# Flamingo layer with a mixture of experts: the up products of the routed experts take the rows' high and low parts in one product

## What is computed

```python
x = x + tanh(g_xattn) * cross_attention(layernorm(x), ctx, Wq, Wk, Wv)
h = layernorm(x)
top, ids = top_k(h @ router_w.T, 1)
xs = h * sigmoid(top)
for e in range(8):
    g, u = split(xs @ w_gate_up[e])
    routed = where(ids == e, (silu(g) * u) @ w_down[e], routed)
x = x + tanh(g_ffn) * (routed + shared_expert(h))
```

## Time and profile before

| | us |
|---|---|
| median of 3 runs | 973.37 (971.97 to 973.90) |
| profiled execution | 973.49 |
| its span in the profile | 971.3 |
| TensorE busy in the span | 944.4 |
| VectorE busy | 628.1 |
| ScalarE busy | 548.8 |
| first gate product of unit 0 starts at | 699.0 |

### The profile page before, as it was taken

One profiled execution on the slowest core, in us unless ns is written; L12 is line 12 of the kernel. 1 busy time (PEld: TensorE's weight loads), 2 busy tenths in 40 slices (PEclk: granted clock), 3 DMA queues, 4 the chain that ended last, 5 costly groups with the idle time before them and its releaser, 6 DMA issues. The chain is left out here.

```text
span 971.3 us, 24842 instructions
## 1 busy us (share of the span) xinstructions
PE 944.4 (97%) x10541; PEld 782.7 (81%) x10541; DVE 628.1 (65%) x1461; ACT 548.8 (57%) x839; POOL 171.6 (18%) x206
## 2 busy tenths in 40 slices
PE   5899999999999999999889999999999999999997
PEld 4677777777777777777777998999988888988886
DVE  6877755867558656676666444344577777777774
ACT  5477766777676777676732121221356666666653
POOL 1002121121112122112242300000111122112111
PEclk9999999999999999999999999999999999999999
DMA  8454544655435745354552310011386787677762
GB/s 314 109 104 99 92 101 93 134 104 97 98 94 132 158 80 116 79 107 127 113 141 94 91 34 32 22 44 57 123 258 214 235 242 233 211 232 243 229 202 64
DMA packets 175403, 129.98 MB, mean 134 GB/s; under 512 B 114610, under 2 KB 152498, under 8 KB 175288
## 3 DMA queue, kind: packets, MB, share of 16 engines
q1 hardware_dynamic: 165864, 108.60, 43.3%
q0 software_dynamic: 6544, 16.46, 5.5%
q10 hardware_dynamic: 2880, 3.29, 1.0%
HBM read 88.79 MB, written 13.56 MB: 105 GB/s over the span
## 5 line engine op out<-in xcount | busy, mean ns | idle before, releaser
L583 PE MATMUL bank<-arena_f32r 128*128 128x512 f32 (+1 forms) x1308 | 331.8, 403 | 12.4 <-DVE arena_f32r L946 12.0
L583 PEld LDWEIGHTS bank<-arena_f32r 128*128 128x128 f32 (+1 forms) x1308 | 231.9, 184 | 75.4 <-DVE arena_f32r L898 10.6
L777 ACT ACTIVATE probs<-score_banks 128x1600 f32<-128x1600 f32 x96 | 144.9, 1509 | 46.5 <-PE score_banks L602 45.9
L1689 ACT ACTIVATE hT_hi<-arena_f 128x224 fp32r<-128x224 f32 (+2 forms) x96 | 42.3, 441 | 116.9 <-DVE arena_f L1700 116.9
L1628 PE MATMUL bank<-xnT,arena_f32r 128*128 128x224 f32 (+1 forms) x720 | 102.5, 293 | 0.0
L1628 PEld LDWEIGHTS bank<-xnT,arena_f32r 128*128 128x128 f32 x720 | 97.0, 190 | 1.8 <-issue 0.7
L1700 DVE TENSOR_TENSOR arena_f<-bank,arena_f 128x224 f32<-128x224 f32 (+2 forms) x93 | 41.2, 443 | 65.8 <-PE bank L1628 65.1
L617 PEld LDWEIGHTS bank<-probs,values 128*17 128x17 f32 (+1 forms) x3072 | 63.4, 97 | 23.4 <-issue 21.5
L617 PE MATMUL bank<-probs,values 128*17 128x100 f32 (+1 forms) x3072 | 78.8, 250 | 0.8 <-ACT probs L777 0.8
L1054 POOL TENSOR_TENSOR heads_out<-heads_out,inv_sum 100x256 f32<-100x256 f32 x30 | 30.3, 1010 | 209.2 <-DVE inv_sum L1017 209.2
L1590 DVE TENSOR_TENSOR arena_f32r<-arena_f,arena_f32r 128x1024 fp32r<-128x1024 f32 x43 | 52.6, 1224 | 18.8 <-ACT arena_f32r L1583 18.8
(11 more groups left out here) (282 smaller groups left out, 1803.7 us busy)
## 6 DMA issues: line engine op xcount, KB each, us to landing
arena_f<-L_ffn_w_gate_up SPq DMA_DIRECT2D x48, 512.0 KB, 4.0
arena_f<-L_ffn_w_down SPq DMA_DIRECT2D x24, 512.0 KB, 4.0
arena_f<-ctx SPq DMA_DIRECT2D x15, 722.0 KB, 4.2
w_raw<-L_ffn_w_gate_up SPq DMA_DIRECT2D x16, 512.0 KB, 3.8
w_raw<-L_ffn_w_down SPq DMA_DIRECT2D x8, 512.0 KB, 5.0
x_all<-x SPq DMA_DIRECT2D x8, 400.0 KB
x_rows<-x_all SPq DMA_DIRECT2D x4, 800.0 KB
x_all<-x_rows POOLq DMA_DIRECT2D x4, 768.0 KB, 6.5
```

The lines of the kernel that those rows point to most:

```text
L583: product = PE.matmul(bank[0:rows, :], src[:, j, 0:rows], weight, start=(m == 0), stop=(m == 11))
L777: A.activation(k.probs[n % 2][:], k.score_banks[:, :, 0:GH * k.N].rearrange("p j (r n) -> p j r n", r=GH), ACT.Exp, scale=float(HD) ** -0. ...
L1689: A.activation(k.hT[it % 2][0][:, j, 0:width], k.hidden[j][:, 0:width], ACT.Copy).then_inc(r.h_high, 1)
```

## The change

The up product gets the form of the gate product: `pe_expert_gate` becomes `pe_expert_gate_up` and is called for both. For each of the two blocks in a unit there are now a copy by ScalarE of the bank's second half to the tile `up_first` (`act_copy_up`), and an addition by VectorE (`dve_sum_up`); the multiplication reads `up_first` and not the bank (`dve_mult_expert`), and waits for the addition. `up_first` is one tile for both blocks, so the copy of a block waits for the multiplication before it (`r.mult`). The order on VectorE changes: the sums of block 1 come before the low part of block 0, and the residual addition moves from the end of quarter 0 to the middle of quarter 1. The rest of the diff takes cases out of `pe_gate_up` that its remaining callers in the shared stage don't have.

```diff
-def pe_expert_gate(k, r, PE, w, n, j):
+def pe_expert_gate_up(k, r, PE, w, n, j, which):
     it, u, xs = r.it0 + n, r.u0 + n, k.xn_both[n // k.NQ % 2]
-    bank = k.bank[product_bank(r, it, j, 0)]
-    high, low = (t[:].rearrange("p (k f) -> p k f", k=k.KD)[:, :, P * j:P * j + P] for t in k.w_split[u % 3][0])
-    w.wait_ge(r.w_low, 3 * u + 1)
+    bank = k.bank[product_bank(r, it, j, which)]
+    high, low = (t[:].rearrange("p (k f) -> p k f", k=k.KD)[:, :, P * j:P * j + P] for t in k.w_split[u % 3][which])
+    w.wait_ge(r.w_low, 3 * u + which + 1)
     if n:
-        w.wait_ge(r.gate_summed, 2 * n + j - 1)
+        w.wait_ge((r.gate_summed, r.up_summed)[which], 2 * n + j - 1)
     else:
-        w.wait_ge(r.silu, 2 * it)
+        w.wait_ge((r.silu, r.mult)[which], 2 * it)
...
+def act_copy_up(k, r, A, w, n, j):
+    it = r.it0 + n
+    w.wait_ge(r.gu, 4 * it + 2 * j + 2)
+    w.wait_ge(r.mult, 2 * it + j)
+    A.activation(k.up_first[:, 0:SLOTS], k.bank[product_bank(r, it, j, 1)][:, SLOTS:2 * SLOTS],
+                 ACT.Copy).then_inc(r.up_copied, 1)
...
+def dve_sum_up(k, r, V, w, n, j):
+    up = k.up_first[:, 0:SLOTS]
+    w.wait_ge(r.up_copied, 2 * n + j + 1)
+    V.tensor_tensor(up, k.bank[product_bank(r, r.it0 + n, j, 1)][:, 0:SLOTS], up, ADD).then_inc(r.up_summed, 1)
+
+
+def dve_mult_expert(k, r, V, w, n, j):
+    h, it = k.hidden[j][:, 0:SLOTS], r.it0 + n
+    w.wait_ge(r.silu, 2 * it + j + 1)
+    w.wait_ge(r.up_summed, 2 * n + j + 1)
+    V.tensor_tensor(h, k.up_first[:, 0:SLOTS], h, MULT).then_inc(r.mult, 1)
...
         for j in range(KF):
-            pe_expert_gate(k, r, PE, w, n, j)
-            pe_gate_up(k, r, PE, w, r.it0 + n, r.u0 + n, j, 1, k.xnT[e % 2], SLOTS)
+            for which in range(2):
+                pe_expert_gate_up(k, r, PE, w, n, j, which)
...
         act_copy_gate(k, r, A, w, n, 0)
         if a is not None:
             act_part_high(k, r, A, w, a)
+        act_copy_up(k, r, A, w, n, 0)
         act_silu_expert(k, r, A, w, n, 0)
         act_copy_gate(k, r, A, w, n, 1)
         act_h_high(k, r, A, w, r.it0 + n, 0, SLOTS)
+        act_copy_up(k, r, A, w, n, 1)
         if b is not None:
             act_part_high(k, r, A, w, b)
         act_silu_expert(k, r, A, w, n, 1)
...
         dve_sum_gate(k, r, V, w, n, 0)
         if a is not None:
             dve_part_low(k, r, V, w, a)
-        dve_mult(k, r, V, w, r.it0 + n, 0, SLOTS)
+        dve_sum_up(k, r, V, w, n, 0)
+        dve_mult_expert(k, r, V, w, n, 0)
+        dve_sum_gate(k, r, V, w, n, 1)
+        dve_sum_up(k, r, V, w, n, 1)
         dve_h_low(k, r, V, w, r.it0 + n, 0, SLOTS)
-        dve_sum_gate(k, r, V, w, n, 1)
         if b is not None:
             dve_part_low(k, r, V, w, b)
-        dve_mult(k, r, V, w, r.it0 + n, 1, SLOTS)
+        dve_mult_expert(k, r, V, w, n, 1)
+        if e and q == 1:
+            dve_add_residual(k, r, V, w, e - 1)
         dve_h_low(k, r, V, w, r.it0 + n, 1, SLOTS)
         if n == 0 and r is k.first:
             dve_shared_add(k, V, w, 15, shared_points(16))
         if c is not None:
             dve_part_low(k, r, V, w, c)
-        if n and q == 0:
-            dve_add_residual(k, r, V, w, e - 1)
```

More of the change, by code:

```diff
@@ L348, in sweep_semaphores @@
     r.gate_copied, r.gate_summed = sem(f"{name}_gate_copied"), sem(f"{name}_gate_summed")
+    r.up_copied, r.up_summed = sem(f"{name}_up_copied"), sem(f"{name}_up_summed")
     r.ids_in = sem(f"{name}_ids_in")
@@ L1607, in pe_gate_up @@
     taken = (r.silu, r.mult)[which]
-    if it < min(r.it0, CT) and j == 0:
+    if it < CT and j == 0:
         weight = [t[:] for t in k.w_first[which]]
@@ L1612, in pe_gate_up @@
         w.wait_ge(r.w_low, 3 * u + which + 1)
-    if r.it0 and it == 0:
+    if it == 0:
         if j == 0:
@@ L1617, in pe_gate_up @@
             w.wait_ge(k.first_copied, which + 1)
-    elif r.it0 and it == 1:
+    elif it == 1:
         w.wait_ge(k.exped, 6 * k.B)
-    elif it <= r.it0:
-        if r.it0 and it == 2:
+    else:
+        if it == 2:
             w.wait_ge(k.finish_v, 4)
-        w.wait_ge(taken, 2 * it + (j if it < r.it0 else 0))
-    else:
-        w.wait_ge(taken, 2 * it + j - 1)
+        w.wait_ge(taken, 2 * it + j)
     for i in range(k.KD * share // shares, k.KD * (share + 1) // shares):
@@ L2205, in sweep_again @@
     k.G.dma_reset()
-    for s in [r.w_high, r.w_low, r.gu, r.gate_copied, r.gate_summed, r.silu, r.mult, r.h_high, r.h_low, r.routed_down, r.ids_in, r.xt_turned,
+    for s in [r.w_high, r.w_low, r.gu, r.gate_copied, r.gate_summed, r.up_copied, r.up_summed, r.silu, r.mult, r.h_high, r.h_low, r.routed_down, r.ids_in, r.xt_turned,
               r.xt_high, r.xt_low, r.y_added, *r.w_in, *r.rows_in, *r.residual_in, *r.y_out]:
```

## The result

The changed kernel takes 979.80 us (median of 5 runs, 978.95 to 982.51) against 973.07 before: a ratio of 1.0072, 95% interval 1.0061 to 1.0083, so 6.7 us slower. (The 973.07 is the median of five runs; the 973.37 of the first three is within 0.3 of it.) The forecast was 976.6, slower, with a range of 971.5 to 980.5. The direction and the cause hold; the loss is twice what the sum gave.

What follows compares the result with a forecast made beforehand. TensorE bounds at 32.72 us per four units; after the change VectorE and ScalarE at 33.05 against 32.08. Last part b 3.3 us later, less 0.16 for shorter products: 3.2 on the profiled 973.49, less 0.12: 976.6 us, range 971.5 to 980.5.

Steps and rivals of the forecast that it cites:

- 1.1 us of room in four units: Routed stage before the change: VectorE's own pace is 31.6 us for four units, against TensorE's 32.72.
- The product is 0.08 us shorter: TensorE's up product in the gate's form: each costs 0.08 us less, 64 of them 5.1 us.
- The formula for the products' spacing: N / 2.4 + 2.5 ns for a TensorE product of N columns; estimated saving 0.6 us in all; profile row preferred.
- The second copy of up: ScalarE's block 1 copy between VectorE's multiplication and part b: 0.25 us more a round, bounds 0.24 and 0.36.
- 0.41 us for the sum of block 0: VectorE's up sum ahead of the multiplication: 0.38 + 0.03 us more a unit, bounds 0.30 and 0.46.
- The tail: After unit 31's last up product: the hidden values' low part is done some 0.4 us early, so the tail holds.
- The residual addition: On VectorE, moved to quarter 1 between multiplication and part c: costs 0.14 us in place of 1.32.
- Rival 1: TensorE stays the bound, faster: 968.3 us; points are rounds of 7.72 or 7.82, new steps 0.42 to 0.52; chance 0.13.
- Rival 3: Longer VectorE and ScalarE round: a copy not overlapping and a handoff twice as long, 0.1 more, 979.5 us; chance 0.08.

Runs made afterwards that it cites:

- product alone: Changed kernel without the low rows' share of the up product: TensorE's new form only, no copy or sum of up, old order elsewhere; 969.1 us, ratio 0.9948.
- the two moves: Changed kernel with block 1's up copy ahead of block 0's high part, and block 0's up copy and sum ahead of weights' part a; 969.11 us, ratio 0.9962.
- copy ahead: Changed kernel with up copied to the hidden tiles' free halves, block 1's copy ahead of block 0's high part on ScalarE; 971.38 us, ratio 0.9987.
- sum ahead: Changed kernel with block 0's up copy and sum ahead of the weights' part a on ScalarE and VectorE; 972.99 us, ratio 1.0001.

## Why the prediction was right, and where it fell short

- **TensorE bounds before, with 1.1 us of room in four units.** Right. The product alone gained its 4 us, and an addition of 1.2 us per expert cost nothing before and everything after.
- **The product is 0.08 us shorter, 5.1 us in all.** Right: with nobody in the way four units take 32.07 us and the stage is 5.3 us shorter. The medians of the two kernels that reach this pace show 3.7 and 4.0 us; in the one with the product alone the stage began 1.45 us later than in the profile of before (700.42 against 698.97), ahead of anything that was changed.
- **The formula for the products' spacing** (the Trainium skill, TensorE: Matmul & The Clock Gate, Back-to-back issue gap). The measured saving, 5.3 us in the stage, stands with the rows, not with the 0.6 us that the formula gives.
- **The second copy of up costs 0.25 in the round.** Right: 2.04 us from multiplication to part b, 0.24 for a copy added at that place.
- **The step that failed: 0.41 us for the sum of block 0.** It measured 0.49. I took the handoff from an operation that waits for one semaphore, while this multiplication waits for two; with one it is 0.42. The round is 8.05 and not 7.96, the last up product of block 0 starts at 961.55 in place of 959.27, 2.3 us later.
- **The tail.** I had 0.4 us to spare ahead of the last down product. There was none:

```profile
967.74 0.39 DVE L1725 TENSOR_TENSOR arena_f32r<-arena_f,hT_hi 128x224 fp32r<-128x224 f32 x1 [0.46 <-ACT hT_hi L1709]
```

```profile
968.25 0.17 PEld L1735 LDWEIGHTS score_banks<-wdown_hi,hT_hi 128*112 128x112 f32 x1 [0.32 <-issue]
```

  The low part ends at 968.13, the last down product's weights load at 968.25, and TensorE's loads idled 0.32 us before that. The profile names no releaser; by the times it was this low part. What went wrong is that I let ScalarE take the copy of the last up product as soon as the product was done. Its last matmul ends at 965.57 (965.31 and 0.26), and the copy (L1663) starts at 965.92, since block 0's high part (L1709) stands ahead of it on ScalarE and waits for VectorE, which is still behind in unit 31. These 0.35 us are most of what I had to spare:

```profile
965.62 0.39 ACT L1709 ACTIVATE hT_hi<-arena_f 128x224 fp32r<-128x224 f32 x1 [0.21 <-DVE arena_f L1683]
965.92 0.34 ACT L1663 ACTIVATE arena_f<-bank 128x224 f32<-128x224 f32 x1
```

  From the last up product of block 0 to the last addition it took 9.78 us, as before 9.70, where my two shorter products had made it 9.54. Another 0.3 us lie after the last addition and 0.2 outside the span, in one execution each. With 2.3 + 0.2 + 0.5 the 3.0 us between 976.7 and the profiled 979.66 are accounted for. Of the 2.3 us the second wait makes about 2.0 (0.07 in each of 29 rounds; taking it away gained 1.9); the rest is 0.01 here and there in a round and was not taken apart.
- **The residual addition.** It costs 0.12 in place of 1.32 in the changed kernel (0.14 forecast). Right.
- **Rival 1, TensorE stays the bound.** It fell for this order, and it is what the two moves bring about: a round with both steps out of the way. Its point was new steps of at most 0.42 to 0.52 us. With one of them out, four units take 32.39 us (copy ahead) and 32.58 (sum ahead); with both, TensorE's 32.07. The copy ahead also answers the higher of its two points, a round of 7.82 with the expert's extras caught up elsewhere: its round is 7.80, and the extras came through whole. The rule of the Trainium skill to improve the engine with the highest occupancy first (Perfetto Trace Analysis, Identifying the Most-Contended Engine) picked the right engine before the change. How near the next bound was, 1.1 us in four units, did not show in the shares of 65% and 57% against 97%.
- **Rival 3, a longer round.** In number this is the nearest: it had 0.1 more in a round and 979.5, and 0.09 more came. Of its two reasons one holds, the longer handoff (0.10 after the sum's end, where I had 0.03); the copy did overlap. I gave it 0.08 of the chances.

The two single moves gained more than forecast. By the rounds they are right: the copy ahead took 33.37 - 32.39 = 0.98 us off four units, 0.25 a round as expected, and the sum ahead 0.79, where I had 0.76. By the stage alone they gained 7.8 and 6.1 us, where I had 7.2 and 5.7; the remainder of 0.5 lies at the stage's ends and was not taken apart.

## What to carry to other kernels

When the bound engine is saturated, ask for the pace of the others by themselves: find a stretch where they are behind and never wait for the bound engine, and measure one round there. Busy shares count neither the waits inside a hand-over chain nor the places where more work is free: here the same copy cost nothing ahead of one operation and 7 to 8 us ahead of another. And a bound that has moved can leave the old one looking busy all the time, when it waits too briefly to be called idle. So in a kernel like this one new work belongs where its engine idles, before an operation that waits, and never between the two halves of a hand-over; a consumer is best put one long operation behind its producer on the same engine.

## What the runs showed of the hardware

A VectorE operation that waits for the one right ahead of it on its own engine starts 0.04 us after its end when that is its only wait, and in the changed kernel 0.10 after it, when it waits for a second semaphore too, here one that has long been raised (the silu that this multiplication waits for ends a microsecond earlier). Between starts that is 0.49 against 0.42 us, once in a unit, worth 1.9 us in all. The multiplication before the change waited for two semaphores as well and showed nothing of it (1.13 us behind part a, as other operations): there a long operation stood ahead of it. Why the second wait costs time was not looked into.
